# Down weights split one operand per half unit, resolvent scalings on ScalarE, largest kernel entry by TensorE

## What is computed

```
xn = layernorm(x)
K  = S4 kernel of length 1024: Cauchy sums over 64 states at 1024 roots, then ifft
y1 = causal convolution of each row of xn with K, plus D * xn
y2 = (silu(xn Wg^T) * (xn Wu^T)) Wd^T      # Wg, Wu: 2752x1024, Wd: 1024x2752
Wg, Wu, Wd = (4-bit words - zero) * scale, one scale and zero per 64 inputs
out = x + y1 + y2
```

## Time and profile before

| | us |
|---|---|
| median of 3 runs (1497.01 to 1501.25) | 1499.83 |
| the profiled execution | 1495.27 |
| its span, first to last instruction | 1493.5 |
| busy in the span: PE | 1333.8 |
| DVE | 957.6 |
| POOL | 674.7 |
| ACT | 457.3 |

### The profile page before, as it was taken

One profiled execution on the slowest core, in us unless ns is written; L12 is line 12 of the kernel. 1 busy time (PEld: TensorE's weight loads), 2 busy tenths in 40 slices (PEclk: granted clock), 3 DMA queues, 4 the chain that ended last, 5 costly groups with the idle time before them and its releaser, 6 DMA issues. The chain is left out here.

```text
span 1493.5 us, 17048 instructions
## 1 busy us (share of the span) xinstructions
PE 1333.8 (89%) x6299; PEld 630.9 (42%) x6299; DVE 957.6 (64%) x1057; ACT 457.3 (31%) x801; POOL 674.7 (45%) x484
## 2 busy tenths in 40 slices
PE   1557899988998999989999999449999999999998
PEld 1423444433443444434444444124444444444444
DVE  4744478899999898678898988535233332432341
ACT  3533444434444354444444543221000000000000
POOL 3642466766678688687978786341000000000000
PEclk9978999999999999999999999769999999999999
DMA  5301554343433344344444443779756236335431
GB/s 177 86 29 70 225 166 131 125 133 115 132 124 117 131 134 140 124 139 134 142 134 141 139 137 112 233 247 365 248 185 222 92 109 221 92 110 196 126 101 57
DMA packets 164646, 218.09 MB, mean 146 GB/s; under 512 B 41426, under 2 KB 121940, under 8 KB 162644
## 3 DMA queue, kind: packets, MB, share of 16 engines
q1 hardware_dynamic: 163988, 209.86, 42.8%
q10 hardware_dynamic: 576, 7.14, 1.4%
HBM read 139.64 MB, written 77.34 MB: 145 GB/s over the span
## 5 line engine op out<-in xcount | busy, mean ns | idle before, releaser
L1310 PE MATMUL px<-xo,wo 128*128 128x512 f16 x2016 | 473.9, 389 | 59.1 <-ACT py L960 30.2
L1310 PEld LDWEIGHTS px<-xo,wo 128*128 128x128 f16 x2016 | 200.1, 100 | 308.7 <-issue 26.5
L684 POOL TENSOR_TENSOR wo<-wf,wo 128x512 f16<-128x512 f32 x147 | 236.5, 1619 | 71.9 <-ACT wo L918 71.9
L703 POOL TENSOR_TENSOR hs<-hf,hs 128x512 f16<-128x512 f32 x154 | 210.8, 1375 | 103.2 <-ACT hs L953 96.1
L1394 PE MATMUL px<-wd,hr 128*128 128x512 f16 x1056 | 235.0, 382 | 10.7 <-DMA wd<-w_d 10.7
L1310 PE MATMUL pz<-xo,wo 128*128 128x512 f16 x1008 | 233.6, 382 | 0.0
L1394 PEld LDWEIGHTS px<-wd,hr 128*128 128x128 f16 x1056 | 102.6, 98 | 131.1 <-DMA wd<-w_d 11.2
L1310 PEld LDWEIGHTS pz<-xo,wo 128*128 128x128 f16 x1008 | 99.5, 99 | 120.8 <-issue 4.6
L1925 DVE SCALAR_TENSOR_TENSOR acc<-px,acc 128x512 f32<-128x512 f32 x32 | 22.1, 691 | 155.3 <-PE px L1394 151.3
L953 ACT ACTIVATE hs<-hf 128x512 f16<-128x512 f32 x154 | 94.5, 621 | 80.8 <-DVE hf L1569 48.2
L693 POOL TENSOR_TENSOR ds<-wf,ds 128x512 f16<-128x512 f32 x69 | 104.2, 1511 | 33.1 <-ACT ds_more L939 20.1
(11 more groups left out here) (211 smaller groups left out, 1406.5 us busy)
## 6 DMA issues: line engine op xcount, KB each, us to landing
h_d<-hs SPq DMA_DIRECT2D x154, 256.0 KB, 3.7
hr<-h_d SPq DMA_DIRECT2D x56, 704.0 KB, 4.2
w_d<-ds SPq DMA_DIRECT2D x69, 256.0 KB, 3.9
wd<-w_d SPq DMA_DIRECT2D x4, 2816.0 KB, 12.5
sz<-in_sz_gate SPq DMA_DIRECT2D x21, 512.0 KB
sz<-in_sz_up SPq DMA_DIRECT2D x21, 512.0 KB
sz<-in_sz_down SPq DMA_DIRECT2D x20, 512.0 KB
xc_d<-xo SPq DMA_DIRECT2D x8, 1024.0 KB, 10.5
```

What stands on the lines that cost most here:

```text
L684: pool.tensor_tensor(w_dest(t, j, 1), w_place_of(j), w_dest(t, j, 0), ALU.subtract).then_inc(wlo_done, 1)
L703: pool.tensor_tensor(hs[:, j, :, 1, :], h_place_of(p, j), hs[:, j, :, 0, :], ALU.subtract)\
L1310: done = pe.matmul(bank[:, :], wo[t % 2][:, j, wp, k * P:(k + 1) * P], xo[p][:, j, xp, k, :], start=(j in (0, 3) and k == 0 and wp == 0 an ...
```

## The change

1. `down_step(n, i)` on each engine puts one split of the down weights into each half i of each unit n, from unit 3 on: step t = 2(n-3)+i does split t, 77 in all, the last (the tail's T2) at unit 41. The half slabs of group g are dequantized at steps 7g-2 and 7g. The tail becomes group 10 in this row, in `wf[:, 1]`. Nothing of the down weights is left behind unit 41. The slabs' order (`SLABS`) follows from it, and each load is issued where the slab two before it is done.
2. The store buffers `ds` of the splits are three in turn (before two, and four more at the end).
3. `load_wd(j)` is one DMA of 2.8 MB for each j (before, j = 0 to 2 were two DMAs each, the larger one on ScalarE's queue). Now j = 0 is on SP, 1 to 4 on ScalarE's queue, 5 and 6 on SP, all at other places of the program. `wd[0]` to `wd[4]` change places in memory.
4. `up_nibble` in units 4g and 4g+2 moves behind `snap_u2`.
5. The resolvents take place in every second unit from 6 to 20, and three of the ten VectorE instructions of each (scalings by a per-partition number) become ScalarE instructions (`scale_angles`).
6. The largest kernel entry: VectorE reduces the kernel's rows to 8 numbers, PE broadcasts them by one small matmul, VectorE reduces again. GpSimd's reduction over partitions goes.

```diff
+def split_step(n, i):
+    return 2 * (n - 3) + i
+def half_steps(t):
+    if t % 7 == 5:
+        return [(t // 7 + 1, 0)] if t // 7 + 1 <= NG else []
+    if t % 7 == 0:
+        return [(t // 7, 1)] if t // 7 <= NG else []
+    return []
...
 # GpSimd
+            def down_step(n, i):
+                t = split_step(n, i)
+                for g, h in half_steps(t):
+                    if g == NG:
+                        pool.wait_ge(dlo_done, split_place(NG - 1, T2 if h else T4) + 1)
+                        pool.memset(wf[0:P - TB, 1, h, 1, :], 0.0).then_inc(wzero_done, 1)
+                if 0 <= t < SPLITS:
+                    d_low(t // 7, D_ORDER[t % 7])
...
 # VectorE
+            def down_step(n, i):
+                t = split_step(n, i)
+                for g, h in half_steps(t):
+                    down_words(g, h)
+                if t % 7 == 1 and 0 <= t // 7 <= NG:
+                    d_sum(t // 7, T1)
+                    d_sum(t // 7, T3)
+                if t % 7 == 3 and 0 <= t // 7 <= NG:
+                    d_sum(t // 7, T2)
+                    d_sum(t // 7, T4)
...
 # ScalarE, d_high
-                if SPLIT_TURN[q]:
-                    act.wait_ge(ds_out[split_slot(q)], 16 * SPLIT_TURN[q])
+                if q >= 3:
+                    act.wait_ge(ds_out[q % 3], 16 * (q // 3))
...
 # ScalarE, units 41 to 43
             silu_tail(41)
-            load_wd(0)
...
+            load_wd(1)
+            load_wd(2)
             h_high(NG, 0, A12)
             h_high(NG, 0, A22)
-            d_high(NG, T1)
-            d_high(NG, T2)
-            down_nibble(NG - 1, 0)
-            silu_tail(42)
-            load_wd(1)
-            d_high(NG - 1, B11)
             h_high(NG, 0, S1)
             h_high(NG, 0, S2)
-
-            down_nibble(NG - 1, 1)
+            silu_tail(42)
+            h_high(NG, 0, S4)
             snap_s1(43)
...
 # VectorE, resolvent(m)
-                dve.wait_ge(angle_in, 16 * (m + 1))
-                if m >= 2:
-                    dve.wait_ge(cauchy_done, m - 1)
+                dve.wait_ge(numer_done, 1)
+                dve.wait_ge(scaled_done, m + 1)
-                dve.tensor_scalar(re, co, sc[:, 3:4], None, ALU.mult)
-                dve.tensor_scalar(im, si, sc[:, 2:3], None, ALU.mult)
-                link(dve.tensor_scalar(res, co, sc[:, 5:6], None, ALU.mult))
...
 # ScalarE, every second unit
+                act.activation(re, co, ACT.Copy, scale=sc[:, 3:4])
+                act.activation(im, si, ACT.Copy, scale=sc[:, 2:3])
+                act.activation(res, co, ACT.Copy, scale=sc[:, 5:6]).then_inc(scaled_done, 1)
...
 # SP, behind the last store_h of unit 40
+            sp.wait_ge(wlo_done, 7 * 21 + 3)
+            load_wd(0)
+            for j in (A12, A22, S1, S2, S4):
+                store_h(NG, 0, j)
             sp.wait_ge(prod_done, products_before(42))
             load_hr(0, 0, 0)
             load_hr(0, 0, 1)
```

More of the change, by code:

```diff
@@ L84, with _slabs, down_slab, slab_arrived @@
 PHASE_A = products_before(NU)
+def split_step(n, i):
[6 more added lines that the diff above has]
+    return []
+def _slabs():
+    order = [("gate", 0), ("up", 0), ("gate", 1), ("up", 1)]
+    for n in range(2, 42):
+        if n == 2 or (n >= 4 and n % 2 == 0 and n < 40):
+            order.append(("gate", n // 2 + 1))
+        if n == 40:
+            order.append(("gate", 21))
+        for i in range(2):
+            if i == 1 and n >= 4 and n % 2 == 0 and n < 40:
+                order.append(("up", n // 2 + 1))
+            if i == 0 and n == 3:
+                order.append(("up", 2))
+            for g, h in half_steps(split_step(n, i)):
+                order += [("down", g, h)] if g < NG else [("tail", 0, h), ("tail", 1, h)]
+    return order
+SLABS = _slabs()
+SLAB = {s: m for m, s in enumerate(SLABS)}
+NIBBLES = [sum(s[0] != "tail" for s in SLABS[:m + 1]) for m in range(len(SLABS))]
 def slab_gate(t):
[L89 removed]
+    return SLAB["gate", t]
 def slab_up(t):
[L93 to L101 removed]
+    return SLAB["up", t]
+def down_slab(g, kh, half):
+    return SLAB["down", g, half] if g < NG else SLAB["tail", kh, half]
+def slab_arrived(m):
+    return sum(64 if s[:2] == ("tail", 0) else 32 for s in SLABS[m % 2:m + 1:2])
 def split_place(g, j):
[L106 removed]
+    return 7 * g + D_POS[j]
 def sum_place(g, j):
[L111 to L131 removed]
+    return 4 * g + T_POS[j]
+SPLITS = 7 * (NG + 1)
 def conv_pieces(sp_, i):
@@ L376, in load_tail, with load @@
                                  z[:, None, :].broadcast_to((n // 32, 32, 1024))).then_inc(slab_in[slot], 16)
+            def load(m):
+                if m >= len(SLABS):
+                    return
+                kind, a = SLABS[m][:2]
+                if kind == "gate" and a == 21:
+                    load_slab(m, raw_v, sz_v)
+                elif kind == "gate":
+                    load_slab(m, raw_gate[a], sz_gate[a])
+                elif kind == "up":
+                    load_slab(m, raw_up[a], sz_up[a])
+                elif kind == "down":
+                    h = SLABS[m][2]
+                    load_slab(m, raw_down[a, :, h * 512:(h + 1) * 512], sz_down[a, h])
+                else:
+                    load_tail(m, a, SLABS[m][2])
+            def down_step(n, i):
+                t = split_step(n, i)
+                for g, h in half_steps(t):
+                    load(down_slab(g, 0, h) + 2)
+                    if g == NG:
+                        load(down_slab(g, 1, h) + 2)
+                if 1 <= t <= SPLITS:
+                    store_w((t - 1) // 7, D_ORDER[(t - 1) % 7])
             def store_h(g, p, j):
@@ L491, in _ @@
-                if g == 6:
+                    for h in range(2):
+                        sp.dma_start(kpad[h:h + 1, 0:P], zrow[0:1, :]).then_inc(kpad_out, 16)
+                if g == 7:
                     sp.wait_ge(krow_done, 1)
                     sp.dma_start(kpad[:, P:].rearrange("n (b a) -> b n a", b=M8), krow[:, :, :]).then_inc(kpad_out, 16)
+            load(slab_gate(21) + 2)
             for j in (S1, S2, S4):
                 store_h(NG - 1, 0, j)
-            load_tail(1, 0)
+            down_step(40, 0)
@@ L601, in _ @@
                     .then_inc(kshift_in, 16)
-            load_wd(2, KC - 2, KC)
+            sp.wait_ge(prod_done, PHASE_A)
+            load_hr(0, 1, 0)
             sp.wait_ge(xc_out, 16 * 8)
             load_xc(0, 0, 0)
+            load_hr(0, 1, 1)
+            sp.wait_ge(hf_done, 88)
+            for i in range(3):
+                sp.wait_ge(ds_out[i], 16 * ((SPLITS - 1 - i) // 3 + 1))
+            load_acc(0, 0)
+            load_acc(0, 1)
+            for j in L_ORDER[:2]:
+                store_h(NG, 1, j)
             load_hr(0, 2, 0)
@@ L762, in _ @@
                 w_low(2, j)
+            down_step(3, 1)
             c22(3)
@@ L908, in down_nibble @@
                     act.wait_ge(dlo_done, split_place(g - 1, T2 if h else T4) + 1)
-                nibble(slab_down(g, h), wf[:, 1, h, :, :])
+                nibble(SLAB["down", g, h], wf[:, 1, h, :, :])
             def w_high(t, j):
@@ L1495, in down_words @@
                     dve.wait_ge(dlo_done, split_place(g - 1, T2 if h else T4) + 1)
-                dequantize(slab_down(g, h), wf[:, 1, h, :, :])
+                if g < NG:
+                    dequantize(SLAB["down", g, h], wf[:, 1, h, :, :])
+                else:
+                    tail_words(0, h)
+                    tail_words(1, h)
             def tail_words(kh, h):
-                m = slab_tail(kh, h)
+                m = SLAB["tail", kh, h]
                 slot = m % 2
```

437 lines of the change are left out of this document (176 added, 261 removed).

## The result

The changed kernel takes 1535.2 us (median of 4 runs, 1531.8 to 1540.0) against 1498.5 for the kernel before on the same chip: a ratio of 1.0245, 95% interval 1.0209 to 1.0281. It is slower by 37 us, where 1438 was predicted. The profiled execution has a span of 1535.7 us, 42 more than before.

What follows compares the result with a forecast made beforehand. It saw 48 us lost at the turn, from late down weights queued on ScalarE, and 50.5 in stage A; 1495.3 - 45 - 15 = 1435, 1439 against the median, stated as 1438, range 1408 to 1472.

Steps and rivals of the forecast that it cites:

- The turn: Between stage A's last full unit and the first down products: 48 us lost, of which the change gives back 45.
- (b): At the turn: hr, issued about E+24 (E: end of unit 40) behind 5.6 MB of weights, should land just in time.
- rival 3: The turn's hole stays in part, from blocked ScalarE or late weights and hr: gain 22, median 1462; 0.12 with Rival 5.
- (a): At the turn: `load_wd(2)` waits on ScalarE for the last split's store; fits barely or is a few us late.
- The evenly spread splits: Stage A units: more split and slab work, 0.55 us of VectorE per unit, bringing it to 17.1 of 18.13 us.
- triples: Three slabs in a row at four places in stage A; VectorE stands about 3.7 us at each.
- Up nibble later: Last 22 units of stage A: ends the wait at the copy of `u`; 8 of 15 us of loss left.
- Resolvents: Units 6 to 21: work spread over 16 units, 1.9 us of VectorE each; 20 us lost, plus 4 for the roots.
- rival 4: Stage A: engines wait for each other in a loop, each unit grows; decides from a 20.7 us period, median 1512; 0.05.
- Rival 5: A slab or store waits in SP's one queue, splits fall into the turn; time of rival 3; 0.12 with it.
- Rival 1: Stage A at its limit: VectorE and GpSimd share one resource, moved work adds 22 us; median 1452; 0.17.
- rival 2: VectorE catches up on the 14.0 us basis, stage A loses only 15; 1414, median 1418; 0.24.

Runs made afterwards that it cites:

- e5: Changed kernel with down halves that fell in even units taken half a unit later, same work and bytes: 1511.9 us, 1.0085 of the kernel before.
- e1: Changed kernel loading only one partition of words and scales from the seventh slab on, all waits and queue orders kept: 1492.1 us (one run).
- e10: Kernel of e9 with SP's stores put ahead of the slab loads that wait for VectorE: 1487.6 us, 0.9928 of the kernel before.
- e7: Kernel before with the resolvent part of the change alone; splits, slabs and turn as before: 1488.5 us, 0.9923 of the kernel before.
- e3: Changed kernel with the eight 1 MB xc stores issued one per group instead of all ahead of unit 2: 1533.1 us, 1.0244 of the kernel before.
- e9: Changed kernel with e5's edit, later down-weight loads at the turn, five xc stores later, unit 2's h sums before its down slab: 1495.0 us, 0.9975.
- e14: Kernel of e10 without VectorE's three instructions on the down slabs of groups 1 to 9; weights then wrong: 1467.6 us (one run).
- e2: Changed kernel without six of the seven VectorE instructions that remained in each resolvent: 1520.5 us (one run).

## Why the prediction was wrong

- **What bounds the kernel** was read rightly: the hole at the turn, and a second loss in stage A.
- **The turn, 45 us.** It gave 31. The step "I give the new waits 3 us" was mis-sized: they were 17. The prediction named the cause itself in (b), hr behind the 5.6 MB of `wd[1]` and `wd[2]`, and then judged by the DMA share of the old stretch (0.64); after, the share was 1.0. PE came to stage B at E + 39 as worked out (1034.8, E being 995.9), but hr, put at E + 24, was issued at E + 40, behind five stores that took 26 us to issue. The 11 MB of rival 3 were the right sum, and (a), the last split's store, cost nothing.
- **The evenly spread splits.** The work was right (17.1 us of VectorE per unit, 17.06 measured). What failed is the sentence on triples: "these cost only where VectorE is already behind", since "a lag of VectorE costs PE nothing up to roughly 13 us". I looked at the slab's wait on VectorE alone. ScalarE waits for the same slab, at its nibble, in order ahead of `silu_first` and `snap_u3`, and its slack to PE is a few us (6.27 us of waiting, 1.49 on PE). I counted four places; there are ten. Moving the halves gave back 24 us of the 57 (e5); e1, which also takes bytes and store waits away, gave 35. Stores issued late, for which stage A had no term, gave 7 (e10).
- **The slack of 13 us** was the distance between two products and not that along ScalarE's queue: hidden operands and splits that wait for VectorE stand ahead of PE's copies, so a lag arrives: in e7 a unit with 22.76 us of VectorE work takes 23.31.
- **Up nibble later** was booked as a gain of 7 us. PE's wait at `u` of the earlier trace rows fell from 20.6 to 11.9 us over the 36 stretches, and one of 28.4 came at the next copy.
- **Resolvents** were a gain, as said. The forecast was 20 us lost in units 6 to 21 and 4 for the roots; alone (e7) it is 28.4 with the roots in it, and in the changed kernel 46.0. It averaged over two units, and light units give nothing to heavy ones.
- **The head** had no term at all: 17 us. The up slab and the first down slabs had moved behind 8 MB of xc stores: moving the stores gave 10.7 of them (e3). A down slab ahead of the h sums on VectorE may have its part, but e9 changed both, and no run shows it alone. The prediction listed what each step issues, but not what the slab order moves at its start.
- **Rivals.** The direction and the period are those of rival 4 (20.7 us decides; 20.9 was measured in the late units, 21.1 over the 36 stretches: 758.70 / 36), which put the kernel at 1512 with a full gain at the turn. Its mechanism, a loop near saturation, is not what ran: VectorE had 18% idle, and at slabs it waited for loads (20 us) and for one weight split (3.8), never for GpSimd's splits of down weights, the link that rival 4 began with. Whether other links between the engines make up the part left open by e14 is not shown. Rival 5 had the mechanism, a slab in one queue and stores behind it, and priced it only at the turn. Rival 1 had two full engines; VectorE and GpSimd were busy 17.06 and 15.35 us of 20.9 per unit, and less VectorE work gave 12 to 17 us (e2) and, without the down slabs' arithmetic, 21 (e14 against e10). Whether the two exclude each other, as the Trainium skill has it (SBUF — State Buffer, section Who interferes with whom), no run here tells.
- **Slips in the sums** that move nothing: rival 2 takes 46 for a turn of 45; the two triples at 3.7 us each are booked as 6; stage A's terms add up to 34 and not 35.

## What to carry to other kernels

With two slots, a load is asked for when the piece before the last is done; list for each piece that time, its landing (9 us here) and every engine that comes to it, and ask what stands behind it on each, not only on the busiest. Averages over units or over an engine's share don't show such waits: late units with VectorE and GpSimd 82% and 73% busy lost 13% of their time. Where loads are moved to fill a hole, divide the bytes wanted by the rate measured when the DMA engines are full (410 GB/s here) and put the small ones that gate others first.
